# Attention scores on one core: bf16 three-part stacks of 72 rows against two-part fp32r stacks of 26 rows per head, placed in 32-row groups of the array

## The chip, the cores and the metric

The kernel runs on one core of a Trainium2 chip. The metric is the device time of one execution in microseconds (us); lower is better.

## The reference

One layer: attention, layer norm, a mixture of experts (8 routed, 2 chosen, 1 shared), layer norm. Input `x` is (8, 512, 128) in float32.

```python
qkv = (x @ w_qkv + b_qkv).reshape(B, 16, S, 24)          # 16 heads of 8, B=8, S=512
q, k, v = jnp.split(qkv, 3, axis=-1)
attn = softmax(einsum('bhqd,bhkd->bhqk', q, k) / sqrt(8))
vals = einsum('bhqk,bhkd->bhqd', attn, v).transpose(0, 2, 1, 3).reshape(B, S, 128)
x = layernorm(x + vals @ w_out + b_out)
# then the mixture of experts on x, and a second layernorm
```

The reshape makes a "head" out of 32 neighbouring tokens of 128 values, so a tile of 128 tokens holds the whole of 4 heads with 512 queries and 512 keys each.

## The kernel before

The work is cut into 32 tiles of 128 tokens (four heads each, `QUADS`), and the engines' programs are written out by hand as a pipeline of stages. The first part of the kernel (attention) ends at about 508 us; the experts and the last norm follow and are not touched.

A stage `(b, i)` works on several tiles at once, each at another step. With q = 4b + i:

- Tile q + 4: its x is transposed (`xT`, slot 4) and multiplied to Q and K (`qkv`, slot 6). ScalarE copies the product to `qk32`, GpSimd splits it into parts of lower precision (`parts`, L814 to L820).
- Tile q + 3: SyncE (SP) stores `parts` to DRAM (L745), waits for that store, and loads it back as two operand stacks `qs` and `ks` (L756, L760). TensorE waits for all of these loads (`stack_loaded`) at the start of the next stage.
- Tile q + 2: scores A. TensorE multiplies (L980) into `scoreA`, and VectorE takes the maximum over the keys (L923, 1024 values per partition and instruction). The negated maxima become two further rows of `qs` (`m2`, L596 and L598, sent by ScalarE's DMA queue, L898).
- Tile q: scores B with the maxima subtracted (L994), with keys on the partitions, into `scoreB`; ScalarE takes the exponential (L889).
- Tile q - 1: probabilities times V (L1014, float32, four heads in four 32-column groups of the array), "PV" below.

A stage has 8 slots (`at`). In each slot TensorE issues two matmuls A and two matmuls B; after that come the jobs of the slot through one shared bank (`pe_job`: xT, qkv, mT, valsT, proj, oT, x1T, gate, counts), and in odd slots PV. `scoreA` has two halves, so the A of a slot waits for the maximum of two slots before (`max_done`); B waits for the exponential of the matmul two before (`exp_done`). VectorE also does the norm statistics and, from stage 8 on, the routing (`choose`, `place`). Each engine executes its own program strictly in order.

A score product in float32 quality is made in bf16 of three parts of q and k: six products of parts, stacked along the contraction dimension, 3 x 24 = 72 rows (B: 74, with the maxima). One SP load makes one band of rows for all four heads, 8 loads per tile.

## Time and profile before

| what | value |
|---|---|
| median of 3 runs | 753.06 us (752.21 to 755.68) |
| span of the profiled execution | 752.8 us |
| TensorE (PE) busy in the span | 671.8 us, 89% |
| VectorE (DVE) busy | 542.0 us, 72% |
| ScalarE (ACT) busy | 433.5 us, 58% |
| GpSimd (POOL) busy | 286.4 us, 38% |
| mean share of the DMA engines in the stretch 126 to 473 us | 37% |

Busy times of an engine are sums of its instructions without overlap. A matmul's row gives its latency, which overlaps with the next matmul: what it occupies is the distance between two starts. The shares are means over stages with different limits, so the stretches have to be read one by one.

### The profile page before, as it was taken

The numbers are of one execution on the slowest core, as the hardware profiler recorded it, in microseconds if no ns is written. First come the engines' busy times: TensorE is split into PE (matmuls) and PEld (weight loads), VectorE is DVE, ScalarE is ACT, GpSimd is POOL, SyncE is SP. The second block draws the span as 40 slices with busy tenths as digits, with TensorE's granted clock in tenths as the row PEclk, the third lists the DMA queues.
The fourth block names the chain that finished last, engine by engine and source line by source line (L and its number), as shares of the span: only waits on it lengthen the run. The fifth ranks groups of instructions, "written<-read, shape, count | busy, mean of one in ns | idle before, by whom it ended". The sixth has DMA issues, their size and how long they took to land. (4 is left out here: it accounts for less than half of the span.)

```text
span 752.8 us, 17081 instructions
## 1 busy us (share of the span) xinstructions
PE 671.8 (89%) x4621; PEld 322.5 (43%) x4622; DVE 542.0 (72%) x1201; ACT 433.5 (58%) x973; POOL 286.4 (38%) x491
## 2 busy tenths in 40 slices
PE   2899999999999999999999999889989888888334
PEld 1232334334343333333333332328877666666211
DVE  4967777889979979979979989756856444545125
ACT  1066677676767667767667776744325444544106
POOL 2133132223434333343352352242435555555506
PEclk9999999999999999999999999999999999999758
DMA  4357776543342342343243241050122222222044
GB/s 79 78 131 153 151 146 114 107 96 68 74 106 53 66 112 60 55 113 70 48 102 90 46 88 55 3 152 22 40 58 66 63 62 62 63 63 58 13 168 168
DMA packets 161848, 62.57 MB, mean 83 GB/s; under 512 B 110586, under 2 KB 155516, under 8 KB 161808
## 3 DMA queue, kind: packets, MB, share of 16 engines
q1 hardware_dynamic: 154112, 48.55, 29.2%
q0 software_dynamic: 5648, 13.26, 6.0%
q10 hardware_dynamic: 2048, 0.27, 0.3%
q8 instruction: 20, 0.33, 0.2%
q14 instruction: 20, 0.16, 0.1%
HBM read 38.04 MB, written 24.26 MB: 83 GB/s over the span
## 5 line engine op out<-in xcount | busy, mean ns | idle before, releaser
L923 DVE TENSOR_REDUCE mx<-scoreA 128x2 f32<-128x1024 f32 x256 | 305.7, 1220 | 66.7 <-PE scoreA L980 64.2
L889 ACT ACTIVATE prob<-scoreB 128x512 f32<-128x512 f32 x512 | 279.3, 600 | 115.9 <-PE scoreB L994 111.4
L980 PE MATMUL scoreA<-ks,qs 72*128 72x512 bf16 x512 | 205.2, 408 | 12.2 <-DMA ks<-parts_dram 9.6
L994 PE MATMUL scoreB<-qs,ks 74*128 74x512 bf16 x512 | 200.3, 394 | 6.3 <-ACT prob L889 3.0
L1014 PE MATMUL pvp<-prob,v 128*32 128x512 f32 x1024 | 138.1, 612 | 0.8 <-ACT pv_sb L881 0.8
L980 PEld LDWEIGHTS scoreA<-ks,qs 72*128 72x128 bf16 x512 | 50.9, 102 | 152.8 <-DVE mx L923 73.6
L1136 POOL DMA_INDIRECT y_dram<-prob x72 | 70.2, 975 | 72.8 <-ACT prob L1290 58.2
L814 POOL CAST parts<-qk 128x256 bf16<-128x256 f32 x32 | 12.6, 395 | 214.0 <-ACT v_raw L563 195.2
L994 PEld LDWEIGHTS scoreB<-qs,ks 74*128 74x128 bf16 x512 | 49.7, 98 | 101.9 <-ACT prob L889 79.7
L488 POOL DMA_INDIRECT slots_dram<-rows,slot_i x64 | 63.3, 989 | 27.2 <-issue 17.7
L1245 DVE TENSOR_TENSOR prob<-scoreA,prob 128x256 f32<-128x256 f32 x72 | 30.6, 425 | 46.3 <-ACT prob L1284 46.3
L1284 ACT ACTIVATE prob<-scoreA 128x256 f32<-128x256 f32 x72 | 27.6, 383 | 39.4 <-PE scoreA L1386 37.7
L1407 PE MATMUL scoreB<-w,prob 128*128 x288 | 44.1, 276 | 0.1
L1290 ACT ACTIVATE prob<-scoreB,prob 128x128 f32<-128x128 f32 x72 | 26.4, 367 | 23.1 <-PE scoreB L1407 23.1
L1407 PEld LDWEIGHTS scoreB<-w,prob 128*128 128x128 f32 x288 | 37.8, 192 | 0.3 <-issue 0.3
L1384 PE MATMUL scoreA<-w_high,ebT_high 128*128 x72 | 35.2, 489 | 2.7 <-issue 1.7
L1232 DVE TENSOR_TENSOR ebT_low<-scoreA,ebT_high 128x128 fp32r<-128x128 f32 x72 | 20.8, 291 | 22.8 <-ACT ebT_high L1274 21.7
L1501 PE MATMUL scoreA<-prob,ident 128*128 128x512 f32 x28 | 15.1, 708 | 23.1 <-DMA prob<-y_dram 23.1
L1366 PE MATMUL scoreA<-ident,prob 128*128 128x128 f32 x72 | 22.6, 316 | 14.5 <-DMA prob<-slots_dram 14.1
L1014 PEld LDWEIGHTS pvp<-prob,v 128*32 128x32 f32 x1024 | 20.5, 109 | 29.3 <-issue 27.7
L1512 ACT ACTIVATE prob<-prob 128x128 f32<-128x128 f32 x32 | 13.2, 482 | 32.9 <-POOL prob L1491 32.9
L1250 DVE COPY prob<-pvp 128x256 f32<-128x256 f32 x72 | 29.9, 415 | 0.6 <-PE pvp L1394 0.6
(177 smaller groups left out, 911.4 us busy)
## 6 DMA issues: line engine op xcount, KB each, us to landing
qs<-parts_dram SPq DMA_DIRECT2D x96, 96.0 KB
parts_dram<-parts SPq DMA_DIRECT2D x32, 192.0 KB, 3.7
slots_dram<-blank POOLq DMA_DIRECT2D x9, 520.0 KB
prob<-slots_dram SPq DMA_DIRECT2D x72, 65.0 KB, 1.8
ks<-parts_dram SPq DMA_DIRECT2D x64, 64.0 KB
prob<-y_dram SPq DMA_DIRECT2D x8, 512.0 KB, 4.4
ks<-parts_dram SPq DMA_DIRECT2D x32, 96.0 KB
xin<-in_L_attn_x SPq DMA_DIRECT2D x32, 64.0 KB, 2.1
```

What stands on the lines that cost most here:

```text
L488: pool.indirect_dma_start(slots_dram, bass.IndirectOffsetOnAxis(ap=slot_i[:, j, t:t + 1], axis=0), rows[:, t, j, :], None).then_inc(scatte ...
L889: act.activation(prob[:, i % 2, j, 2 * u + c, :], scoreB[:, c], ACT.Exp, scale=SCALE).then_inc(exp_done, 1)
L923: dve.tensor_reduce(mx[:, i % 2, at // 2, at % 2 * 2:at % 2 * 2 + 2], scoreA[:, at % 2], AX.X, ALU.max).then_inc(max_done, 1)
L980: ins = pe.matmul(scoreA[:, at % 2, c], qs[0:KR, st, j, qc * P:(qc + 1) * P], ks[0:KR, st, j, :], start=True, stop=True)
L994: pe.matmul(scoreB[:, c], ks[0:KM, i, j, kc * P:(kc + 1) * P], qs[0:KM, i, j, :], start=True, stop=True).then_inc(b_ready, 1)
L1014: ins = pe.matmul(pvp[32 * h:32 * h + 32, :], v[:, (i - 1) % 2, h, j, :], prob[:, (i - 1) % 2, h, j, :], start=(j == 0), stop=(j == 3))
L1136: pool.indirect_dma_start(y2_dram, bass.IndirectOffsetOnAxis(ap=yrow_i[:, r:r + 1], axis=0), yo[:, r, :], None, bounds_check=TOP_K * TILES ...
L1245: dve.tensor_tensor(gated[:, r % 2, :], scoreA[:, 0, r % 2, F:2 * F], silu[:, r % 2, :], ALU.mult) \
L1250: dve.tensor_copy(gatedT[:, (r - 1) % 2, :], pvp[:, 0:F]).then_inc(gT_copied, 1)
L1284: act.activation(silu[:, r % 2, :], scoreA[:, 0, r % 2, 0:F], ACT.Silu).then_inc(silu_done, 1)
L1384: pe.matmul(h, ebT_high[:, r % 2, 0:P], high, start=True, stop=False)
L1407: ins = pe.matmul(y, gatedT[:, r % 2, c * P:(c + 1) * P], w2_flat[:, bass.ds(e * NFC * D + c * D, D)], start=(c == 0), stop=(c == NFC - 1))
```

## The change

q and k are split into two fp32r parts instead of three bf16 parts. Three products of parts are stacked: 24 rows per head (B: 26 with the maxima) instead of 72. Each head's stack lies in its own 32 partitions (`GROUP`), so that the four heads lie beside each other in `qs` and `ks`, and a score matmul uses 32 rows of the array's 128. The two A matmuls of a slot are now those of two heads (2 and 3 in slots 0 to 3, then 0 and 1), each in its own row group, and are issued one behind the other; the two B matmuls (of one head) follow. GpSimd's split has two instructions instead of four. SP makes the stacks with 16 loads of 8 or 16 rows per tile instead of 8 of 8 to 24 rows. Not shown: the maxima's two rows are written as fp32r, and the four memsets that put ones into `ks` cover 128 partitions of 512 float32 values instead of 32 partitions of 2048 bf16 values.

```diff
@@ -110,12 +110,9 @@
-    KR = 9 * HD
-    PR = 3 * HD
-
-    K_ROWS = [(0, 0, 3), (PR, 1, 3), (PR + 2 * HD, 0, 1), (2 * PR, 2, 3), (2 * PR + HD, 0, 2)]
-    STACK_DMAS = 3 + len(K_ROWS)
+    KR = 3 * HD
     KM = KR + 2
+    GROUP = 32
     NE = E + 1
...
@@ -139,7 +136,7 @@
-        parts_dram = nc.dram_tensor("parts_dram", (2, 2, 4, 3, P, 32), BF16).ap()
+        parts_dram = nc.dram_tensor("parts_dram", (2, 2, 4, 2, P, 32), F32).ap()
...
@@ -169,12 +166,14 @@
         qk32 = sb("qk32", [P, 2, 4, 32])
-        qkr = sb("qkr", [P, 2, 4, 32])
-        parts = sb("parts", [P, 2, 4, 3, 32], BF16)
-        qs = sb("qs", [P, 4, 4, 512], BF16)
-        ks = sb("ks", [P, 4, 4, 512], BF16)
+        parts = sb("parts", [P, 2, 4, 2, 32], F32R)
+        qs = sb("qs", [P, 4, 512], F32R)
+        ks = sb("ks", [P, 4, 512], F32R)
+
+        STACK = ((0, qs, 0, 0, 1), (0, qs, HD, 0, 2), (1, ks, 0, 0, 2), (1, ks, 2 * HD, 0, 1))
+        STACK_DMAS = 4 * len(STACK)
         mx = sb("mx", [P, 2, 4, NCH])
-        m2 = sb("m2", [16, 2, P], BF16)
+        m2 = sb("m2", [16, 2, P], F32R)
...
@@ -743,7 +743,7 @@
                     need(sp, stack_loaded[par], 16 * STACK_DMAS * (2 * b + (i + 3) // 2))
                     sp.dma_start(parts_dram[par].rearrange("k h i p t -> p (k h i) t"),
-                                 parts[:].rearrange("p k h i t -> p (k h i) t")).then_inc(parts_stored, 16)
+                                 parts[:].rearrange("p k h i t -> p (k h i) t").bitcast(F32)).then_inc(parts_stored, 16)
                     need(sp, parts_stored, 16 * (n + 1))
                     if has(b, i, -1):
...
@@ -752,14 +752,11 @@
                     if isinstance(b, int) and n < 4:
                         sp.wait_ge(ones_set, n + 1)
-                    for r in range(3):
-                        sp.dma_start(qs[PR * r:PR * (r + 1), st],
-                                     parts_dram[par, 0].rearrange("h i (d c) t -> (i d) h (c t)", d=HD)) \
-                          .then_inc(stack_loaded[par], 16)
-                    for row, i0, i1 in K_ROWS:
-                        sp.dma_start(ks[row:row + HD * (i1 - i0), st],
-                                     parts_dram[par, 1, :, i0:i1].rearrange("h i (d c) t -> (i d) h (c t)", d=HD)) \
-                          .then_inc(stack_loaded[par], 16)
+                    for k, to, row, i0, i1 in STACK:
+                        for h in range(4):
+                            sp.dma_start(to[GROUP * h + row:GROUP * h + row + HD * (i1 - i0), st].bitcast(F32),
+                                         parts_dram[par, k, h, i0:i1].rearrange("i (d c) t -> (i d) (c t)", d=HD)) \
+                              .then_inc(stack_loaded[par], 16)
...
@@ -812,12 +809,8 @@
                     need(pool, parts_stored, 16 * n)
                     need(pool, split_done, n)
                     pool.tensor_copy(parts[:, :, :, 0, :], qk32[:]).then_inc(split_step, 1)
-                    need(pool, split_step, 3 * n + 1)
-                    pool.tensor_tensor(qkr[:], qk32[:], parts[:, :, :, 0, :], ALU.subtract).then_inc(split_step, 1)
-                    need(pool, split_step, 3 * n + 2)
-                    pool.tensor_copy(parts[:, :, :, 1, :], qkr[:]).then_inc(split_step, 1)
-                    need(pool, split_step, 3 * n + 3)
-                    pool.tensor_tensor(parts[:, :, :, 2, :], qkr[:], parts[:, :, :, 1, :], ALU.subtract) \
+                    need(pool, split_step, n + 1)
+                    pool.tensor_tensor(parts[:, :, :, 1, :], qk32[:], parts[:, :, :, 0, :].bitcast(F32), ALU.subtract) \
                         .then_inc(split_done, 1)
                 if isinstance(b, int) and q == -4:
                     columns_of_blanks()
...
@@ -920,8 +913,9 @@
                 for at in range(8):
                     if has(b, i, 2):
                         dve.wait_ge(a_ready, 8 * (q + 2) + at + 1)
-                        dve.tensor_reduce(mx[:, i % 2, at // 2, at % 2 * 2:at % 2 * 2 + 2], scoreA[:, at % 2], AX.X,
-                                          ALU.max).then_inc(max_done, 1)
+                        h = FIRST_A[at // 4]
+                        dve.tensor_reduce(mx[:, i % 2, h:h + 2, at % 4], scoreA[:, at % 2], AX.X, ALU.max) \
+                           .then_inc(max_done, 1)
                     for kind in jobs.at(b, i, at):
                         if kind in ("valsT", "proj", "mT"):
                             dve_job(dve, kind, b, i)
...
@@ -970,17 +964,17 @@
                 if has(b, i, 2):
                     pe.wait_ge(stack_loaded[i % 2], 16 * STACK_DMAS * (2 * b + i // 2 + 2))
-                def score_a(at, c):
+                def score_a(at):
                     if has(b, i, 2):
-                        st, j, qc = (i + 2) % 4, at // 2, at % 2 * 2 + c
-
-                        if c == 0:
-                            need(pe, max_done, 8 * (q + 2) + at - 1)
-                        ins = pe.matmul(scoreA[:, at % 2, c], qs[0:KR, st, j, qc * P:(qc + 1) * P],
-                                        ks[0:KR, st, j, :], start=True, stop=True)
-                        if c == 1:
-                            ins.then_inc(a_ready, 1)
+                        st, qc = (i + 2) % 4, at % 4
+
+                        need(pe, max_done, 8 * (q + 2) + at - 1)
+                        for c in range(2):
+                            g = GROUP * (FIRST_A[at // 4] + c)
+                            ins = pe.matmul(scoreA[:, at % 2, c], qs[g:g + KR, st, qc * P:(qc + 1) * P],
+                                            ks[g:g + KR, st, :], start=True, stop=True)
+                        ins.then_inc(a_ready, 1)
                 def score_b(at, c):
...
@@ -991,14 +985,14 @@
                             pe.wait_ge(m_loaded, 32 * (q + 1))
                         need(pe, exp_done, 16 * q + 2 * at + c - 1)
-                        pe.matmul(scoreB[:, c], ks[0:KM, i, j, kc * P:(kc + 1) * P], qs[0:KM, i, j, :],
+                        g = GROUP * j
+                        pe.matmul(scoreB[:, c], ks[g:g + KM, i, kc * P:(kc + 1) * P], qs[g:g + KM, i, :],
                                   start=True, stop=True).then_inc(b_ready, 1)
                 for at in range(8):
                     j, u = at // 2, at % 2
-                    score_a(at, 0)
+                    score_a(at)
                     score_b(at, 0)
-                    score_a(at, 1)
                     score_b(at, 1)
                     for kind in jobs.at(b, i, at):
                         pe_job(pe, kind, b, i)
```

TensorE's program, the first two slots of a stage, before (L980 is scores A, L994 scores B, L521 the transposed maxima, L1014 PV; in brackets the semaphores it waits for):

```order
L980 MATMUL scoreA<-ks,qs 128x512 [waits max_done,stack_loaded1]
L994 MATMUL scoreB<-qs,ks 128x512 [waits exp_done,m_loaded]
L980 MATMUL scoreA<-ks,qs 128x512
L994 MATMUL scoreB<-qs,ks 128x512 [waits exp_done]
L980 MATMUL scoreA<-ks,qs 128x512 [waits max_done]
L994 MATMUL scoreB<-qs,ks 128x512 [waits exp_done]
L980 MATMUL scoreA<-ks,qs 128x512
L994 MATMUL scoreB<-qs,ks 128x512 [waits exp_done]
L521 MATMUL shared<-ident,mx 16x128 [waits max_done,job_read]
L1014 MATMUL pvp<-prob,v 32x512 [waits v_ready,exp_done]
L1014 MATMUL pvp<-prob,v 32x512 x3
```

and the same place of the changed kernel (L975 is scores A, L989 scores B, L1008 PV):

```order
L975 MATMUL scoreA<-ks,qs 128x512 [waits max_done,stack_loaded1]
L975 MATMUL scoreA<-ks,qs 128x512
L989 MATMUL scoreB<-qs,ks 128x512 [waits exp_done,m_loaded]
L989 MATMUL scoreB<-qs,ks 128x512 [waits exp_done]
L975 MATMUL scoreA<-ks,qs 128x512 [waits max_done]
L975 MATMUL scoreA<-ks,qs 128x512
L989 MATMUL scoreB<-qs,ks 128x512 [waits exp_done] x2
L521 MATMUL shared<-ident,mx 16x128 [waits max_done,job_read]
L1008 MATMUL pvp<-prob,v 32x512 [waits v_ready,exp_done]
L1008 MATMUL pvp<-prob,v 32x512 x3
```

The number of matmuls is the same; the second A of a slot stands ahead of the first B, and no longer behind its wait. SP's program for one tile, before:

```order
L745 DMA parts_dram<-parts 128x24x32
L756 DMA qs<-parts_dram 24x4x512 x3
L760 DMA ks<-parts_dram 24x4x512
L760 DMA ks<-parts_dram 16x4x512
L760 DMA ks<-parts_dram 8x4x512 x2
L760 DMA ks<-parts_dram 16x4x512
```

and in the changed kernel (L757 is the one line of all loads):

```order
L745 DMA parts_dram<-parts 128x16x32
L757 DMA qs<-parts_dram 8x512 x4
L757 DMA qs<-parts_dram 16x512 x4
L757 DMA ks<-parts_dram 16x512 x4
L757 DMA ks<-parts_dram 8x512 x4
```

One load per head and band takes the place of one load per band: 16 issues instead of 8, with 3072 pieces of 128 bytes instead of 9216 of 64.

## Rows read from the trace of the kernel before

**Rows 1.** Busy us (and instructions) by stretch; PEclk, DMA share, GB/s at the end.

```profile
0.00:56.00 56.00, 39.08 (x159) 14.75 (x161) 37.93 (x40) 16.38 (x36) 13.31 (x32) 1.00 0.44 94
56.00:126.00 70.00, 69.69 (x531) 23.88 (x530) 51.77 (x58) 49.90 (x107) 19.77 (x44) 1.00 0.72 144
126.00:473.00 347.00, 343.59 (x2696) 131.35 (x2698) 306.84 (x620) 242.56 (x515) 123.30 (x198) 1.00 0.37 79
```

**Rows 2.** Groups by line, 241 to 299 us: busy us, mean ns, idle before.

```profile
L923 DVE TENSOR_REDUCE mx<-scoreA 128x2 f32<-128x1024 f32 x33 | 39.4, 1220 | 6.0 <-PE scoreA L980 5.5
...
L994 PE MATMUL scoreB<-qs,ks 74*128 74x512 bf16 x64 | 24.6, 384 | 0.4
...
L1014 PE MATMUL pvp<-prob,v 128*32 128x512 f32 x128 | 17.0, 605 | 0.0
```

**Rows 3.** TensorE in order of time, from 306.58 us: start, duration, x instructions.

```profile
306.58 1.07 PE L1014 MATMUL pvp<-prob,v 128*32 128x512 f32 x8
307.58 0.39 PE L980 MATMUL scoreA<-ks,qs 72*128 72x512 bf16 x1
307.80 0.38 PE L994 MATMUL scoreB<-qs,ks 74*128 74x512 bf16 x1
```

**Rows 4.** Groups by line and shape of TensorE, 42 to 57 us.

```profile
L994 PE MATMUL scoreB<-qs,ks 74*128 74x512 bf16 x16 | 10.1, 634 | 0.0
```

**Rows 5.** TensorE in order of time, 57 to 61 us.

```profile
56.98 0.63 PE L980 MATMUL scoreA<-ks,qs 72*128 72x512 bf16 x1
57.41 0.63 PE L994 MATMUL scoreB<-qs,ks 74*128 74x512 bf16 x1
...
58.19 1.94 PE L1014 MATMUL pvp<-prob,v 128*32 128x512 f32 x8
60.05 0.47 PE L980 MATMUL scoreA<-ks,qs 72*128 72x512 bf16 x1
```

**Rows 6.** Busy time and granted clock (PEclk) of two short stretches.

```profile
508.00:510.70 2.70, 1.76 (x12) 1.50 (x12) 0.38 (x2) 2.37 (x3) 0.48 (x4) 1.00 0.03 6
511.00:514.00 3.00, 3.00 (x12) 2.54 (x11) 1.45 (x6) 0.11 (x1) 0.00 (x0) 0.50 0.00 0
```

**Rows 7.** All engines in order of time, 516 us: matmuls of fp32r operands.

```profile
516.23 0.40 PE L1354 MATMUL scoreA<-ebT_high,w_high 128*128 128x512 f32 x1
516.23 0.19 PEld L1355 LDWEIGHTS scoreA<-ebT_high,w_low 128*128 128x128 f32 x1
516.46 0.39 PE L1355 MATMUL scoreA<-ebT_high,w_low 128*128 128x512 f32 x1
```

**Rows 8.** All engines in order of time, 300 to 317 us.

```profile
300.09 0.39 PE L980 MATMUL scoreA<-ks,qs 72*128 72x512 bf16 x1
...
301.72 0.38 SPq L745 DMA_DIRECT2D parts_dram<-parts  x1
...
305.71 1.14 SPq L756 DMA_DIRECT2D qs<-parts_dram  x3
...
306.89 1.94 SPq L760 DMA_DIRECT2D ks<-parts_dram  x5
...
311.56 0.38 PE L509 MATMUL shared<-xT,wq 128*128 128x128 f32 x2
...
313.23 0.28 ACT L563 ACTIVATE v_raw<-shared 128x128 f32<-128x128 f32 x1
...
313.93 0.40 POOL L814 CAST parts<-qk 128x256 bf16<-128x256 f32 x1 [1.21 <-ACT v_raw L563]
...
316.85 0.38 SPq L745 DMA_DIRECT2D parts_dram<-parts  x1
```

**Rows 9.** All engines in order of time, 12 to 18 us.

```profile
13.66 1.83 SPq L760 DMA_DIRECT2D ks<-parts_dram  x5
...
17.72 0.61 PE L980 MATMUL scoreA<-ks,qs 72*128 72x512 bf16 x1 [9.35 <-DMA ks<-parts_dram]
```

**Rows 10.** ScalarE's copy of PV, once a stage; duration min/median/max, first and last start.

```profile
L881 ACT ACTIVATE pv_sb<-pvp x31: 597/597/598, 70.3 to 500.0; 128x512 f32<-128x512 f32 x31
```

More of the change, by code:

```diff
@@ L284, in layer @@
         CHOSEN = 14
+        FIRST_A = (2, 0)
         PLACED = 38
@@ L597, in dve_job @@
                 need(dve, msplit_step, q + 2)
-                dve.scalar_tensor_tensor(m2[:, 1, :], shared[0:16, 0:P], -1.0, m2[:, 0, :], ALU.mult,
+                dve.scalar_tensor_tensor(m2[:, 1, :], shared[0:16, 0:P], -1.0, m2[:, 0, :].bitcast(F32), ALU.mult,
                                          ALU.subtract).then_inc(job_read, 1)
@@ L897, in stage @@
                             for m in range(2):
-                                act.dma_start(qs[KR + m:KR + m + 1, (i + 1) % 4].rearrange("p h x -> p (h x)"),
-                                              m2[:, m, :]).then_inc(m_loaded, 16)
+                                act.dma_start(qs[KR + m::GROUP, (i + 1) % 4].bitcast(F32),
+                                              m2[:, m, :].bitcast(F32)).then_inc(m_loaded, 16)
             run_stages(act, stage)
@@ L951, in _ @@
             dve.memset(v[:], 0.0).then_inc(cleared, 1)
-            dve.memset(ks[64:96, 0], 1.0).then_inc(ones_set, 1)
-            dve.memset(ks[64:96, 1], 1.0).then_inc(ones_set, 1)
+            dve.memset(ks[:, 0].bitcast(F32), 1.0).then_inc(ones_set, 1)
+            dve.memset(ks[:, 1].bitcast(F32), 1.0).then_inc(ones_set, 1)
             dve.memset(half[:], -0.5).then_inc(cleared, 1)
@@ L957, in _ @@
             dve.memset(blank[:], 0.0).then_inc(cleared, 1)
-            dve.memset(ks[64:96, 2], 1.0).then_inc(ones_set, 1)
-            dve.memset(ks[64:96, 3], 1.0).then_inc(ones_set, 1)
+            dve.memset(ks[:, 2].bitcast(F32), 1.0).then_inc(ones_set, 1)
+            dve.memset(ks[:, 3].bitcast(F32), 1.0).then_inc(ones_set, 1)
             dve.wait_ge(cleared, CLEARS)
```

## The prediction

> **What bounds the kernel now.** I read the busy times by stretch first. Between 56 and 126 us TensorE (PE) is busy 69.7 of 70.0 us and VectorE (DVE) 51.8 (74%); between 126 and 473 us, where norms and routing are added, PE is busy 343.6 of 347.0 us and DVE 306.8 (88%) [rows 1]. So PE looks like the only limit, but DVE stands close behind it. ScalarE copies PV once a stage, 31 times from 70.3 to 500.0 us: 14.3 us a stage [rows 10]. The view by lines of four of these stages says who waits: in 58 us the maxima are 39.4 us of DVE's work, and in front of them DVE stands idle 6.0 us, 5.5 of them for scores A [rows 2]. These 6.0 us per four stages are all that a faster PE can give where routing runs; then DVE is the limit.
>
> What PE's time consists of is read from the distances between starts. A score matmul occupies 0.22 us (307.58 to 307.80) and a PV group of eight instructions 1.00 us (306.58 to 307.58) [rows 3]. Per stage: 32 scores are 7.0 us, 4 PV groups 4.0 us, and in the plain stretch (five stages in 70 us, 14.0 each) 3.0 us remain for the jobs.
>
> TensorE's clock decides as much. The page's clock column shows nothing low before 470 us, but the durations do: from 42 to 57 us the scores B take 634 ns [rows 4] against 384 ns later [rows 2], and their starts lie 0.43 us apart [rows 5], twice the 0.22. That is the 1.2 GHz level. PE streamed scores there without a gap and the clock did not rise; it rose behind the first PV group: 58.19 us at the low level, and the next matmul A at 60.05 us is already of the short kind [rows 5]. Near the end it is seen the other way round: from 508 to 510.7 us PE is busy only 1.76 us of 2.70, and in the next row the granted clock is 0.50 [rows 6].
>
> **The change, part by part.**
>
> Rate of fp32r. Matmuls of 512 columns with fp32r operands start 0.23 us apart, their weight loads take 0.19 us and lie under the matmul before them, on the same rows (516.23 and 516.23) [rows 7]. Against 0.22 that is nothing: 32 x 0.01 = 0.3 us a stage, on PE alone.
>
> Two heads at once. The two A of a slot lie in different row groups and write different banks. The trace shows no row groups, but it shows column groups: the eight PV instructions, each over 512 columns, take 1.00 us together [rows 3], where one after another at 0.22 they would take at least 1.76. I take the same for rows. The third group, of the first B, can run beside them or not: a slot then costs between 2 x 0.23 = 0.45 us and 3 x 0.22 = 0.66 us, where it was 0.88; a stage 3.6 to 5.3 us where it was 7.0. If nothing overlaps it stays at 7.4 us (a rival below).
>
> Switching. PV takes 1.00 us at the high clock and 1.86 at the low [rows 3, 5]; with a part that doubles and a part that doesn't, 0.86 doubles and 0.14 is fixed. That fixed part I charge for each change between row groups, column groups and the whole array. Jobs in even slots, and behind the scores in odd ones, now bring about six more: 0.8 us a stage. Net on PE: 7.0 - (3.6 to 5.3) - 0.8 - 0.3 = 0.6 to 2.3 us less a stage. In the plain stretch a stage of PE's own work is then 11.7 to 13.4 us.
>
> The Trainium skill (page "TensorE: Matmul & The Clock Gate", Part 3 on packing) says that a weight load overlaps running matmuls only where the row group differs. The two B of a slot share one; by that rule 8 x 0.19 = 1.5 us a stage would come back and eat most of the gain. The trace disagrees: the load at 516.23 runs under a matmul on the same 128 rows [rows 7], and the measurement decides.
>
> DVE. Number and length of the maxima stay (33 x 1220 ns) [rows 2]. The floor of four stages is 58 - 6 = 52 us. PE will not hide everything: behind slot 6 it has the qkv job and then a PV group before the next A, over 2 us against the 1.22 of a maximum. I take 60% of the 6.0 us: 3.6 us per four stages, and with 347 / 58 = 6 groups **-22 us** (bounds: 0 and -36).
>
> The way of the stacks. From the start of the qkv job in one stage to the matmul two stages later that needs it: 311.56 to 313.93 is 2.4 us to GpSimd's cast; 2.9 to SP's store (316.85); store to first load 4.0 (301.72 to 305.71); eight loads 3.1 (1.14 and 1.94) [rows 8]; last issue to TensorE 2.2 (15.49 to 17.72) [rows 9]. Sum 14.6; qkv stands 11.5 us into its stage (300.09 to 311.56) [rows 8], and 2 x 14.3 - 11.5 = 17.1 are there: 2.5 us to spare. Afterwards: two of four split instructions, -1.4; eight more issues at 0.39, +3.1: 16.3. With qkv about 9 us into a shorter stage (six maxima of 1.22 us and the small jobs between them), a stage can't be shorter than (9 + 16.3) / 2 = 12.7 us. That is under DVE's floor with routing (13.0 and up), so it costs nothing there, but it limits the plain stretch: five stages from 14.0 to 12.7, **-6 us** (0 to -9).
>
> The start. The first A waits for the first stack (17.72) [rows 9]: +3.1 - 1.4 = +1.7 us. The stage of 42 to 57 us, 32 x 0.43 = 13.8 us of scores, falls to 8 slots x 3 x 0.43 = 10.3: -3.4. With the later stacks of the stages between I set the sum to 0 (-2 to +2). The larger memsets, the maxima's two rows and the stored bytes lie off the path; fewer and longer DMA pieces only help (DMA share 0.72 and 0.37) [rows 1]. The last stages have no A: 0.
>
> The clock. With 26 of 128 rows at work and PE waiting for DVE, the array does much less than before, and rows 5 and 6 say that this is what the clock follows. I expect it to fall now and then. Price: at the low level a stage of PE is 8 x (0.86 to 1.29) + 4 x 1.86 + 2 x 3.0 = 20 to 24 us against 13.6, so 7 to 10 us for each stage's worth spent low. I take a stage and a quarter of some 29, in short pieces: **+10 us** (bounds 0 and, all of them low, +200 to +290).
>
> The skill's same page (Part 1, the clock gate) says the grant follows how busy TensorE has been; by it alone a PE above 90% busy would keep its clock, and the sum would be 10 us lower. The row of 42 to 57 us, without a gap at 634 ns, says that busy time alone isn't it [rows 4].
>
> Sum: 752.8 (span; 0.3 us from the median of the runs) - 22 - 6 + 0 + 10 = **735 us**. With the bounds of the first terms and a clock that hardly falls: 708 to 748.
>
> **The rivals.**
>
> Slower, by the clock (0.19). For: the scores were 57% of the array's rows and become 20%, PE gets gaps, and low it stayed through 15 us of dense scores [rows 4]. Against: PV, behind which it rose, stays as it is, and when PE gets slower it has fewer gaps again. It decides from 28 / (7 to 10) = 3 to 4 stages' worth low. Seven stages low give 725 + 50 to 70 = 775 to 795; half of them 830 and more.
>
> Row groups don't run at once (0.08). Then PE keeps its 32 x 0.23 and pays the switches, 0.3 + 0.8 = 1.1 us a stage, in 29 stages +32: 785 us.
>
> The stacks come late (0.07). If a load costs 0.5 us of SP or lands later, the way is 18 us and more, a stage 13.6 to 14.2: 742 to 750 us.
>
> PE's gain is real, but DVE's waits only move to other places (0.06): 749 to 756, no change.
>
> **How the numbers follow.** The forecast holds 0.60. Differences under 0.5% (3.8 us, 749.3 to 756.8) can't be told from none. Faster: 0.60 and 0.04 of the late stacks = 0.64. No change: 0.03 + 0.06 = 0.09. Slower: 0.19 + 0.08 = 0.27. The range runs from 706 (two more than the best forecast) to 800, which leaves out the longer half of the clock's rival and little else.
>
> **What would show it.** Right: both A of a slot starting within 0.2 us of each other, with the next matmul of the whole array at 0.5 to 0.7 us after a slot's start; DVE busy 93% or more between the same stages, its idle time before the maxima near 2.4 us in four stages; plain stages of 12.5 to 13 us; scores of 0.4 us with short stretches of 0.63. Wrong: A starts 0.23 us apart (no overlap); scores and PV at 0.63 and over 1 us for long stretches, and granted clock of 0.5 inside the attention (clock); TensorE waiting for `ks` or `qs` loads at a stage's start (stacks).

## The result

The changed kernel takes 840.94 us (831.8 to 867.63, 4 runs) against 753.02 us before. The ratio is 1.105 [1.0982, 1.1118]: slower; it is taken over fast runs alone, those within 1.5% of the kernel's fastest (here 831.8 and 836.67 us). The forecast was 735 us, range 706 to 800; the time lies outside the range, on the side of the rival "slower, by the clock". The profiled execution is the 831.8 us run, span 830.0 us, beside the span of 752.8 us before.

The page after: engine totals, the slices with TensorE's granted clock, and the groups that answer to [rows 2].

```profile
PE 727.4 (88%) x4621; PEld 360.1 (43%) x4622; DVE 541.9 (65%) x1201; ACT 435.0 (52%) x973; POOL 255.7 (31%) x427
...
PEclk9999999976975998988988965556999999999958
...
L917 DVE TENSOR_REDUCE mx<-scoreA 128x2 f32<-128x1024 f32 x256 | 305.4, 1221 | 122.6 <-PE scoreA L975 120.6
...
L989 PE MATMUL scoreB<-qs,ks 26*128 26x512 f32 x512 | 248.4, 555 | 21.3 <-ACT prob L882 20.7
L1008 PE MATMUL pvp<-prob,v 128*32 128x512 f32 x1024 | 177.7, 775 | 0.8 <-ACT pv_sb L874 0.8
L975 PE MATMUL scoreA<-ks,qs 24*128 24x512 f32 x512 | 142.6, 582 | 15.7 <-DMA ks<-parts_dram 11.9
```

The clock row, in which the page of before has no digit under 9 ahead of its 38th slice (696 us), is now broken from its 9th slice on (166 us). A mean hides this at first sight: PV is 775 ns over the whole span here, where it was 605 in [rows 2]. It is a mixture of about 605 and 1062. By stretches it comes apart:

```profile
56.00:106.00 50.00, 48.52 (x242) 17.00 (x241) 24.72 (x29) 23.63 (x48) 6.32 (x17) 1.00 0.49 108
318.00:369.00 51.00, 48.64 (x421) 21.07 (x417) 44.81 (x91) 36.38 (x79) 14.15 (x23) 1.00 0.27 59
369.00:379.00 10.00, 9.19 (x37) 3.00 (x34) 7.35 (x16) 4.51 (x9) 4.08 (x5) 0.50 0.45 97
495.00:570.00 75.00, 72.48 (x342) 26.06 (x341) 37.98 (x100) 34.37 (x66) 17.59 (x24) 0.50 0.10 23
```

The first of these rows prints 1.00, but that stands there only because the trace has no record of the clock before 106 us; the durations say that it was low (the same trap as in [rows 4] against [rows 1]). TensorE by line and shape, 60 to 100 us of the changed kernel:

```profile
L989 PE MATMUL scoreB<-qs,ks 26*128 26x512 f32 x31 | 19.3, 719 | 1.2 <-ACT prob L882 1.2
L1008 PE MATMUL pvp<-prob,v 128*32 128x512 f32 x64 | 15.5, 1062 | 0.0
L975 PE MATMUL scoreA<-ks,qs 24*128 24x512 f32 x30 | 10.8, 756 | 0.0
```

PV takes 1062 ns and B 719: the 1.2 GHz level until 106 us, where before it ended at 60 us [rows 5]. By the records of the clock it then falls every 20 to 70 us, for 10 to 31 us, and from 495 to 570 us it is low throughout. Of the 513 us from the first to the last of the matmuls below it is low for 226.

Stage lengths are the distances between the starts of the matmul that transposes the maxima (L521), one a stage:

| | before | after |
|---|---|---|
| stages 1 to 6, us | 12.5 15.6 14.3 13.6 13.6 13.6 | 12.9 13.7 20.0 21.1 16.8 13.6 |
| four stages from 326.3 (after) and 287.3 us (before) | 15.5 13.7 15.2 13.7 | 15.0 13.7 16.0 16.7 |
| last three | 15.2 13.2 14.9 | 21.9 19.9 23.1 |
| start of the 7th / 29th / 32nd of these matmuls | 113.1 / 432.9 / 476.2 | 127.9 / 477.9 / 542.8 |
| first matmul of the experts' loop (L1366, now L1360) | 557.3 | 635.4 |

So the 78 us are lost in four places: 14.8 in the first stages, 30.2 over the 22 stages of the middle, 21.6 in the last three, 11.5 behind them, where norms and the last PV still run low. From there to the end both take 195 us. Every stage that is more than 0.3 us longer has a low clock in it. The stages wholly at the high clock take what they took before: 13.6 or 13.7, and at best 0.5 less (15.0 for 15.5).

### The profile page after: what moved, and what is told of

It is laid out like the page before. It is cut to its first block and busy times, and to the rows that moved or that the text cites. A ratio compares the mean times of both kernels' runs of the same rounds, so it can differ in the third digit from the quotient of the medians.

```text
span 830.0 us, 17193 instructions
## 1 busy us (share of the span) xinstructions
PE 727.4 (88%) x4621; PEld 360.1 (43%) x4622; DVE 541.9 (65%) x1201; ACT 435.0 (52%) x973; POOL 255.7 (31%) x427
## 2 busy tenths in 40 slices
DMA packets 119096, 58.65 MB, mean 71 GB/s; under 512 B 79098, under 2 KB 106620, under 8 KB 119056
## 5 line engine op out<-in xcount | busy, mean ns | idle before, releaser
L989 PE MATMUL scoreB<-qs,ks 26*128 26x512 f32 x512 | 248.4, 555 | 21.3 <-ACT prob L882 20.7
L1008 PE MATMUL pvp<-prob,v 128*32 128x512 f32 x1024 | 177.7, 775 | 0.8 <-ACT pv_sb L874 0.8
L975 PE MATMUL scoreA<-ks,qs 24*128 24x512 f32 x512 | 142.6, 582 | 15.7 <-DMA ks<-parts_dram 11.9
L989 PEld LDWEIGHTS scoreB<-qs,ks 26*128 26x128 f32 x512 | 101.5, 225 | 93.1 <-ACT prob L882 77.5
L975 PEld LDWEIGHTS scoreA<-ks,qs 24*128 24x128 f32 x512 | 54.7, 222 | 158.2 <-issue 74.1
L811 POOL CAST parts<-qk 128x256 fp32r<-128x256 f32 x32 | 12.6, 395 | 287.8 <-ACT v_raw L563 266.3
L1284 ACT ACTIVATE prob<-scoreB,prob 128x128 f32<-128x128 f32 x72 | 26.5, 368 | 23.1 <-PE scoreB L1401 22.8
L1008 PEld LDWEIGHTS pvp<-prob,v 128*32 128x32 f32 x1024 | 22.4, 120 | 34.4 <-issue 30.5
L1226 DVE TENSOR_TENSOR ebT_low<-scoreA,ebT_high 128x128 fp32r<-128x128 f32 x72 | 20.9, 291 | 22.9 <-ACT ebT_high L1268 21.6
L1360 PE MATMUL scoreA<-ident,prob 128*128 128x128 f32 x72 | 22.5, 314 | 14.6 <-DMA prob<-slots_dram 14.0
L559 ACT ACTIVATE qk<-shared,bq 128x128 f32<-128x128 f32 x64 | 20.1, 364 | 19.9 <-PE shared L514 14.5
```

Of the source, the lines that this page charges most:

```text
L975: ins = pe.matmul(scoreA[:, at % 2, c], qs[g:g + KR, st, qc * P:(qc + 1) * P], ks[g:g + KR, st, :], start=True, stop=True)
L989: pe.matmul(scoreB[:, c], ks[g:g + KM, i, kc * P:(kc + 1) * P], qs[g:g + KM, i, :], start=True, stop=True).then_inc(b_ready, 1)
L1008: ins = pe.matmul(pvp[32 * h:32 * h + 32, :], v[:, (i - 1) % 2, h, j, :], prob[:, (i - 1) % 2, h, j, :], start=(j == 0), stop=(j == 3))
```

## The experiments

A job's own runs of the kernel before were 756, 776, 775 or 775 us, so only ratios are compared over jobs; stage lengths come from the profiles. Of the runs taken once, stage lengths alone are used. Every stage length is that of one profiled execution.

**e1: rows alone.** The kernel before with its scores over 24 of the 72 rows; nothing else is changed. Two thirds of the products and the maxima's rows are left out.

```diff
-                        ins = pe.matmul(scoreA[:, at % 2, c], qs[0:KR, st, j, qc * P:(qc + 1) * P],
-                                        ks[0:KR, st, j, :], start=True, stop=True)
+                        ins = pe.matmul(scoreA[:, at % 2, c], qs[0:PR, st, j, qc * P:(qc + 1) * P],
+                                        ks[0:PR, st, j, :], start=True, stop=True)
...
-                        pe.matmul(scoreB[:, c], ks[0:KM, i, j, kc * P:(kc + 1) * P], qs[0:KM, i, j, :],
+                        pe.matmul(scoreB[:, c], ks[0:PR, i, j, kc * P:(kc + 1) * P], qs[0:PR, i, j, :],
```

> The kernel before with one thing changed: the score matmuls A and B use rows 0 to 23 of their stacks instead of 72 and 74 (it leaves out two thirds of the products and the maxima); still bf16, still no row groups, the same number of matmuls, columns and loads. Theory (the clock follows how much of the array works, and the changed kernel lost it by its 24 to 26 rows): the clock falls here too, scores of 0.63 us appear in long stretches; as nothing overlaps, a low stage is about 23 us against 14.3, and the time is 830 us or more. Rival (fp32r operands, or the row groups, bring the clock down, not the number of rows): no fall, 750 to 756 us.

Measured: 930.74 us, ratio 1.2093 [1.1991, 1.2195]. TensorE's totals in its windows, and its lines in the same stretch:

```profile
56.00:168.00 112.00, 112.00 (x458) 29.44 (x457) 49.36 (x55) 49.77 (x93) 19.26 (x42) 1.00 0.47 91
L994 PE MATMUL scoreB<-qs,ks 24*128 24x512 bf16 x72 | 45.3, 629 | 0.0
...
L1014 PE MATMUL pvp<-prob,v 128*32 128x512 f32 x144 | 34.8, 1062 | 0.0
```

TensorE has no gap in 112 us, with the instructions of before, and the clock stays low: PV takes 1062 ns, and the 1.00 in the row stands only for want of a record before 168 us. A low stage takes 25.3 us (about 23 forecast). After 168 us the clock alternates, and a plain stage at the high level takes 14.1. bf16, no row groups, no new order: fewer rows are enough to lose the high clock here, and TensorE being busy without a gap did not raise it.

**e14: rows given back.** The changed kernel with scores B over all 128 rows.

```diff
-                        g = GROUP * j
-                        pe.matmul(scoreB[:, c], ks[g:g + KM, i, kc * P:(kc + 1) * P], qs[g:g + KM, i, :],
+                        pe.matmul(scoreB[:, c], ks[:, i, kc * P:(kc + 1) * P], qs[:, i, :],
...
+            dve.memset(qs[:, 0].bitcast(F32), 0.0)
             dve.memset(ks[:, 0].bitcast(F32), 1.0).then_inc(ones_set, 1)
```

(and the same memset for the other three parts of `qs`)

> The changed kernel with scores B over all 128 rows of the stacks instead of the 26 of one head; the sum then holds the scores of the four heads (the probabilities are those of that sum), with the instructions, stacks, loads, maxima and exponentials as in the changed kernel. Theory (the clock follows how many rows are at work, not fp32r, nor the 32-row groups, nor the waits): the clock rises near 60 us as before and stays until the last stages; a stage takes 13.6 to 14.3 us where it is plain; ratio 1.00 to 1.03. It gives no gain over before, since the exponentials hold the scores B back. Rival (fp32r stacks, the paired A or the gaps bring the clock down whatever the rows): above 1.08, with falls as in the changed kernel.

Measured: 808.32 us, ratio 1.0406 [1.0332, 1.048]. The page's clock row and the long stretch of [rows 1]:

```profile
PEclk9999999999999999999999999998999999999858
126.00:473.00 347.00, 345.29 (x2481) 157.56 (x2480) 284.64 (x565) 229.21 (x478) 94.20 (x142) 1.00 0.31 66
```

The clock rises at 63 us (before: 60) and does not fall until 541 us. fp32r, row groups for A, paired A and the loads are those of the changed kernel, so none of them is enough to bring the clock down. The edit does two things, though: it gives rows back, and as B now overlaps with no A, TensorE also has hardly a gap (345.29 of 347 us busy; the changed kernel 48.64 of 51). That it is the closed gaps that hold the clock is not excluded by this run; e1 speaks against it, with no gap in 112 us and the clock low. The forecast of no loss was too good: plain stages take 15.1 us, not 13.6 to 14.3, for B over all rows lies beside no A:

```profile
92.67 0.50 PE L979 MATMUL scoreA<-ks,qs 24*128 24x512 f32 x2
93.10 0.73 PE L992 MATMUL scoreB<-qs,ks 128*128 128x512 f32 x2
93.76 0.50 PE L979 MATMUL scoreA<-ks,qs 24*128 24x512 f32 x2
```

Its B starts 0.43 us behind the A, and the slot takes 1.09 us (92.67 to 93.76), where that of before took 0.88. Its two B over all rows take 0.66 us (93.10 to 93.76), as much as the pair in one row group does (below). This kernel has a high clock and is still slower than before.

**e13: the order alone.** The kernel before with two heads at a time and the order A, A, B, B.

```diff
-                        st, j, qc = (i + 2) % 4, at // 2, at % 2 * 2 + c
+                        st, j, qc = (i + 2) % 4, (2, 0)[at // 4] + c, at % 4
...
                     score_a(at, 0)
-                    score_b(at, 0)
                     score_a(at, 1)
+                    score_b(at, 0)
```

> One part of the change alone: the kernel before (bf16 stacks of 72 rows) with the two A of a slot of two heads and issued one behind the other (A, A, B, B). Theory: every matmul still uses more than half of the array, so the clock stays high from about 60 us on; the order costs or gives nothing that can be told, 748 to 758 us on a chip where before takes 753 (ratio 0.99 to 1.01). Rival (it is the order A, A, B, B with its waits that makes TensorE's clock fall in the changed kernel): falls inside the attention and 5% or more.

Measured: 781.93 us, ratio 1.0087 [1.0055, 1.0119], clock high from 67 us on. With stacks of 72 rows the order has no part in the clock. It costs a little, at the edge of what I expected: plain stages 14.3 instead of 13.6 us.

**e5: the order undone.** The changed kernel, but A, B, A, B.

```diff
-                    score_a(at)
+                    score_a(at, (0,))
                     score_b(at, 0)
+                    score_a(at, (1,))
                     score_b(at, 1)
```

> The changed kernel with the slot's matmuls in the old order: A of the first head, B, A of the second head, B. Read from its stages at the high clock, since the clock falls here too. Theory (a slot at the high clock is long because the two B lie in one row group, each waiting for its own weight load, 0.33 us apart, and because B waits for the exponentials; the A beside them costs nothing): the stages stay within 0.3 us of the changed kernel's 13.6 to 15.0 us. Rival (the second A in front of the first B delays the exponentials and took the gain): stages shorter by 0.5 us or more.

One run of 854.97 us, clock falling as in the changed kernel. Its plain stages at the high clock are 13.5 us, so in the changed kernel the order is not what holds them at 13.6.

**e10, e11, e12: who holds the stage at the high clock.** Shorter exponentials in the changed kernel (e10) and before (e11), shorter maxima in the changed kernel (e12).

```diff
+                                W = 512 if isinstance(b, int) and q < 2 else 256
-                                act.activation(prob[:, i % 2, j, 2 * u + c, :], scoreB[:, c], ACT.Exp,
+                                act.activation(prob[:, i % 2, j, 2 * u + c, 0:W], scoreB[:, c, 0:W], ACT.Exp,
```

```diff
-                        dve.tensor_reduce(mx[:, i % 2, h:h + 2, at % 4], scoreA[:, at % 2], AX.X, ALU.max) \
+                        dve.tensor_reduce(mx[:, i % 2, h:h + 2, at % 4], scoreA[:, at % 2, :, 0:256], AX.X, ALU.max) \
```

> The changed kernel with exponentials of 256 instead of 512 columns from the third tile on (half of the probabilities are left out). Theory: at the high clock TensorE's scores B wait for the exponentials through the two banks of scoreB, and this has taken the place of TensorE's own work as the limit; four exponentials of 0.6 us stand against two slots of 0.66 us. Halved, they are some 0.33 us, and a plain stage that lies wholly at the high clock falls from 13.6 us by 1.0 us or more. Rival (TensorE's own work and switching fill the stage in the changed kernel too): 13.3 to 13.6 us. Both expect a lower clock for much of the time.

> The kernel before with the same halved exponentials. By both theories TensorE's own work is the limit there, and its plain stages stay at 13.4 to 13.6 us. If they fall by more than 0.5 us, the exponentials were part of the limit before the change too, and TensorE was never alone on the path.

> The changed kernel with maxima over 256 instead of 512 keys per head (half of the keys are left out of the maximum). Theory (exponentials limit): plain stages at the high clock stay at 13.4 to 13.6 us, and only the stages with routing, 15.2 to 16 us, get shorter. Rival (the maxima limit through the two halves of scoreA): plain stages fall by 1 us or more.

A plain stage wholly at the high clock takes 12.3 us in e10, 13.0 in e11, 13.6 in e12. The windows of these stages, e10, e11, e12 (PE, PEld, DVE, ACT, POOL busy, as in [rows 1]):

```profile
93.20:105.50 12.30, 11.70 (x107) 4.86 (x106) 10.43 (x13) 6.60 (x22) 2.32 (x4) 1.00 0.64 139
```

```profile
85.20:98.20 13.00, 13.00 (x108) 4.84 (x106) 10.45 (x13) 7.41 (x22) 3.35 (x8) 1.00 0.68 149
```

```profile
156.40:170.00 13.60, 12.64 (x107) 4.97 (x107) 7.94 (x21) 9.94 (x22) 3.66 (x6) 1.00 0.40 81
```

Halved exponentials (384 for 597 ns) take 1.3 us from the changed kernel's stage. Halved maxima take nothing: VectorE's work is down to 7.94 us, and the stage stays. So the exponentials bound the plain stage. With them halved TensorE is busy 11.70 of 12.30 us and is close behind as the next limit. Before, TensorE looks like the limit, busy 13.53 of 13.60 us; but with halved exponentials (e11) the stage fell there too, by 0.6, below the 13.4 to 13.6 that I had put down. The exponentials held it as well.

The second half of what I expected of e12 missed, and it teaches more. A stage with routing should have got shorter with shorter maxima. The same kind of stage, wholly at the high clock, in the changed kernel and in e12:

```profile
326.30:341.30 15.00, 14.57 (x123) 6.76 (x122) 13.70 (x32) 10.31 (x23) 3.67 (x7) 1.00 0.31 62
```

```profile
268.10:283.10 15.00, 14.56 (x123) 6.76 (x122) 8.99 (x30) 10.32 (x23) 3.71 (x7) 1.00 0.33 62
```

VectorE has 4.7 us less to do, and the stage stays at 15.0 us. Of the four kinds of stage that alternate behind 126 us this is the one with the most work for VectorE. VectorE does not bound it. Nor does VectorE bound the shortest kind: it takes 13.7 us in the changed kernel and in e12, and 12.4 in e10.

**e2 and e9: rows without use.** Two extra matmuls of 128 rows ahead of the A of each odd slot (e2); in e9 also three in every slot of the first stages.

```diff
+                        for _ in range(FILLERS[at % 2]):
+                            pe.matmul(scoreA[:, at % 2, 0], ks[:, st, 0:P], ks[:, st, :], start=True, stop=True)
                         for c in range(2):
```

(`FILLERS` is (0, 2); e9 has `range(3 if isinstance(b, int) and b < 1 else FILLERS[at % 2])`)

> The changed kernel with two further matmuls over all 128 rows and columns (fp32r, 512 columns, result overwritten) ahead of the two A of each odd slot, where TensorE otherwise waits about 0.5 us for the exponentials: 8 a stage, 0.22 us each. Theory: the array works more, the clock stays high, and since at the high clock the stages are as long as before (13.6 to 15 us), the time falls from 832 to 752 to 765 us. Rival (the stages are long for another reason, the low clock is only a sign of waiting): 830 us or more, since the work only grows.

> The run with two extra matmuls before the scores A of each odd slot held its high clock from 172 us on, but its stages up to there took 23.5 to 24.5 us. Here the first stages (up to the A of stage (0, 3)) get three extra matmuls of 128 rows in every slot, the rest as in that run. Theory (the clock follows the work of the array's rows): the clock rises in the first stages, before 100 us, and stays; stages as in that run at the high clock, 14.3, 15.9, 14.3 and 16.6; time 770 to 795. It is then still above before, though the clock is high, since the change gives no time back at the high clock and the extra matmuls cost 0.7 us a stage. Rival (the late rise is random, not a matter of the work in the first stages): low until 150 us or later, 825 and more.

e2: 828.83 to 894.45 us, median 861.66 (before 756.13). Expected 752 to 765, missed. Two lines from 60 to 160 us, and the stretch behind the rise:

```profile
L992 PE MATMUL scoreB<-qs,ks 26*128 26x512 f32 x68 | 41.4, 707 | 0.0
L1011 PE MATMUL pvp<-prob,v 128*32 128x512 f32 x128 | 31.0, 1062 | 0.0
172.00:476.00 304.00, 300.45 (x2408) 131.82 (x2404) 256.56 (x501) 207.56 (x433) 85.75 (x130) 1.00 0.32 69
```

Low until 172 us, at 23.5 to 24.5 us a stage, then high for 304 us. e4 below, with the same extra matmuls and a copy on ScalarE, rose at 99 us, and fell again for 120 us at 331: the extra matmuls do not hold the clock reliably. e10, whose first stages are those of the changed kernel, rose at 86 us where that rose at 106. With one profile of each, such moments can't be compared closely. e9: 849.3 us, ratio 1.0989 [1.0904, 1.1075]; the clock rose at 81 us, as expected (beside e4's 99 and e10's 86 that is weak evidence), and fell for 20 us at 217. The time is 54 us above my range: the three extra matmuls made the first stages 17.4 to 21.1 us, so that the sixth of the L521 matmuls starts at 137.9 us (the changed kernel: 114.2). The later ones cost 0.7 us a plain stage (14.3) and more where routing runs, up to 15.1 for 13.7. The last stages were at the high clock, but behind them, between 559 and 589 us, it was low for 27 us. Work added to hold the clock cost what it gave.

**e3: the overlap taken away.** e2 with both A of a slot in the row group of the same head as B.

```diff
-                            g = GROUP * (FIRST_A[at // 4] + c)
+                            g, qc = GROUP * j, at % 2 * 2 + c
```

> As the run with the fillers, but the two A of a slot are again of one head, the same as that of the B of the slot, so that all four lie in one row group and none can overlap. Theory (at the high clock the overlap gives almost nothing, because TensorE waits for the exponentials anyway): within 15 us of the run with the fillers. Rival (the overlap is worth its 0.2 us and more a slot on the path, 1.7 us a stage, and something else took the gain): 50 us or more above it.

1111.11 to 1189.66 us, median 1177.83: my theory, which gave the overlap no worth, missed. Stages at the high clock are 17.5 us and more (e2: 14.3), low ones 31.3 (24.5). The row groups do run at once, and it is worth some 3 us a stage against the same stacks without it. TensorE's four score matmuls of a slot in one row group, with the weight loads (PEld) of the last two:

```profile
331.53 0.73 PE L977 MATMUL scoreA<-ks,qs 24*128 24x512 f32 x2
331.87 0.42 PEld L991 LDWEIGHTS scoreB<-qs,ks 26*128 26x128 f32 x2
332.10 0.63 PE L991 MATMUL scoreB<-qs,ks 26*128 26x512 f32 x2
332.66 0.33 PE L504 MATMUL shared<-ident,xin 128*128 128x128 f32 x1
```

They take 1.13 us, where those of bf16 take 0.88. So of what the overlap gives, a part only makes up for that.

**e4: the exponentials' turn.** e2 with a copy on ScalarE, 0.2 to 0.25 us, between the two exponentials of even slots.

```diff
+                                if u == 0 and c == 1:
+                                    act.activation(extra[:], ident[:, 0:64], ACT.Copy)
```

> As the run with the fillers, with one short ScalarE copy (128x64, some 0.2 us) between the two exponentials of each even slot: 4 a stage, 128 in all. Theory (ScalarE's exponentials, two banks of scores B, are the path through a pair of slots): the whole of it shows, 4 x 0.2 x 29 = 20 to 25 us more than the run with the fillers. Rival (VectorE or TensorE's own work sets the stage): 0 to 5 us more.

824.24 to 873.7 us, median 858.06, which says nothing beside e2's spread. Stages at the high clock 14.8, 16.4, 14.8, 16.6 against e2's 14.3, 15.9, 14.3, 16.6: half of the added 0.8 to 1.0 us in three of four stages, nothing in the fourth, where I had expected the whole. ScalarE is on the path there, but with slack left in places.

**e6, e8: PV between the two B of odd slots,** in the changed kernel (e6) and on e7's kernel (e8), so that ScalarE has work during PV. **e7:** the kernel before with B over 128 rows, the added ones zero.

```diff
+                    if u == 1:
+                        pv(j)
                     score_b(at, 1)
```

```diff
-                        pe.matmul(scoreB[:, c], ks[0:KM, i, j, kc * P:(kc + 1) * P], qs[0:KM, i, j, :],
+                        pe.matmul(scoreB[:, c], ks[:, i, j, kc * P:(kc + 1) * P], qs[:, i, j, :],
...
+            dve.memset(qs[64:128, 0], 0.0)
```

> The changed kernel with PV of an odd slot between the slot's two B instead of behind them and the jobs, so that the exponential of the first B runs under PV. Read from its stages at the high clock. Theory (TensorE and ScalarE wait for each other in a pair of slots: TensorE about 0.5 us for the exponentials in front of B, ScalarE about 1 us during PV): the plain stage falls from 13.6 to 12.4 to 13.0 us. Rival (TensorE's own work or VectorE sets the stage): 13.4 us or more. The clock falls as in the changed kernel or a little less; no time is forecast from it.

> The kernel before with scores B over all 128 rows of the stacks instead of 74; rows 74 to 127 of qs are zeros, so the result is the same, and a matmul takes as long. Theory (the clock follows how much of the array works): it rises soon after the first B, some 42 to 50 us instead of 60, and as TensorE is the limit there, the kernel gains a half of that: 744 to 750 us. Rival (zero rows don't count, or it is PV as such, a float32 matmul, that raises the clock): it rises at 60 us as before, 751 to 754 us.

> As the run with B over 128 rows on the kernel before, with PV of an odd slot between the slot's last A and last B. Theory (in front of B TensorE waits for the exponentials, some 0.2 us twice in an odd slot, and ScalarE stands idle under PV): 0.3 to 0.6 us a stage less, 10 to 20 us below the run without the move. Rival (at the high clock TensorE's own work sets the stage, or VectorE with routing): within 4 us of it.

e6, one run: 1022.12 us, a mean clock of 0.691. Its one stage wholly at the high clock (168.6 to 183.3 us) takes 14.7 us, where the changed kernel's takes 13.6 and I had expected 12.4 to 13.0: a miss. e8: 794.7 us, 1.0207 [1.0135, 1.0279], a miss; plain stages 14.7 instead of 13.6 or 13.7. The place of PV is worse in both by some 1 us, and I did not find out by which wait. e7: 772.19 us, 0.9941 [0.9894, 0.9987]. Its clock was high from 44 to 54 us already, and then from 61 as before; e8, with the same B, shows the same. It is the only version that came out ahead of before, by about half a per cent. That B over 128 rows brings the clock up earlier is suggested by these two, not shown; and the half per cent does not come from there in the profile, where the seventh of the L521 matmuls starts at 113.1 us, as before.

## Why the prediction was wrong

**The clock term (+10) was mis-sized, and that decides.** The price of a low stage was right: 20 to 24 us forecast, 19.9 to 23.1 measured, against 13.6 to 14.9. The extent was not. I took "a stage and a quarter of some 29"; lost are 78 us, 66.6 of them in the stages, at 6.4 to 8.2 us a stage some eight to ten stages' worth, and 11.5 behind the last scores. I had read the right rows ([rows 4] and [rows 5]: 15 us of dense scores without a rise) and said that the array would do much less. Then the sum let it fall "now and then". The step that was missing is a comparison: in the row of 42 to 57 us 72 rows at work and no gap did not raise the clock, and the changed kernel's scores use 24 or 26. PV as such does not hold it up either: e1 has the same PV and 24 rows, and stays low for 112 us. With two thirds of the scores' rows gone a low clock had to be expected for much of the attention (it was 226 of 513 us), not now and then. That fewer rows bring the clock down is shown by e1; e14 brings it back by more rows, with the gaps closed at the same time. The start shows it most plainly. I credited the stage of 42 to 57 us with 3.4 us for shorter scores. It did get 1.9 shorter (15.6 to 13.7), but the rise came 46 us later, and the first six stages together lost 14.8.

The Trainium skill (page "TensorE: Matmul & The Clock Gate", Part 1) ties the grant to how busy TensorE is. Here 112 us with TensorE busy 112.00 of them stayed at 1.2 GHz in e1; setting the rule aside was right, and the consequence was drawn too small. The rival "slower, by the clock" (0.19) is what happened; that the other terms gave nothing back brought the time to its longer half. The bounds 708 to 748 do not come out of the terms, which give 705.8 to 754.8 with a clock that hardly falls. The miss does not hang on that.

**The gain of -22 us (and -6 in plain stages) did not come.** The step that failed is "60% of the 6.0 us", and with it "then DVE is the limit": it assumed that TensorE's shorter slots reach VectorE and that VectorE sets the stage. In e12 the stage with routing kept its 15.0 us with VectorE's work cut from 13.70 to 8.99, and the plain one its 13.6. Two slots of the changed kernel at the high clock, without PV between them, and ScalarE in the same stretch:

```profile
342.54 0.50 PE L975 MATMUL scoreA<-ks,qs 24*128 24x512 f32 x2
342.55 0.49 PE L989 MATMUL scoreB<-qs,ks 26*128 26x512 f32 x1
342.88 0.39 PE L975 MATMUL scoreA<-ks,qs 24*128 24x512 f32 x1
342.88 0.39 PE L989 MATMUL scoreB<-qs,ks 26*128 26x512 f32 x1
342.88 0.39 PE L975 MATMUL scoreA<-ks,qs 24*128 24x512 f32 x1
343.77 0.99 PE L989 MATMUL scoreB<-qs,ks 26*128 26x512 f32 x2 [0.49 <-ACT prob L882]
344.69 0.66 PE L525 MATMUL shared<-ident,pv_sb 128*128 128x128 f32 x4
345.27 1.06 PE L1008 MATMUL pvp<-prob,v 128*32 128x512 f32 x8
346.27 0.50 PE L975 MATMUL scoreA<-ks,qs 24*128 24x512 f32 x2
```

```profile
343.12 2.27 ACT L882 ACTIVATE prob<-scoreB 128x512 f32<-128x512 f32 x4 [0.97 <-PE scoreB L989]
...
346.84 1.09 ACT L882 ACTIVATE prob<-scoreB 128x512 f32<-128x512 f32 x2 [1.45 <-PE scoreB L989]
```

The first slot lasts 342.54 to 342.88, its A and the first B starting within 0.01 us. The second issues its A at 342.88, and then B stands 0.49 us for `prob`: both banks of `scoreB` are full. The two slots end at 344.69, after 2.15 us. The same two slots in the kernel before:

```profile
86.98 0.39 PE L980 MATMUL scoreA<-ks,qs 72*128 72x512 bf16 x1
...
87.86 0.38 PE L980 MATMUL scoreA<-ks,qs 72*128 72x512 bf16 x1
88.28 0.39 PE L994 MATMUL scoreB<-qs,ks 74*128 74x512 bf16 x1
88.50 0.38 PE L980 MATMUL scoreA<-ks,qs 72*128 72x512 bf16 x1
88.77 0.39 PE L994 MATMUL scoreB<-qs,ks 74*128 74x512 bf16 x1
89.00 0.38 PE L525 MATMUL shared<-ident,pv_sb 128*128 128x128 f32 x2
```

2.02 us, 86.98 to 89.00, of which 8 x 0.22 = 1.76 are needed: the B at 88.28 stands 0.42 us behind the A before it, and the one at 88.77 0.27. Such waits are shorter than a matmul's latency, so they hide in TensorE's busy time. Four exponentials take 2.27 us without a gap (343.12), more than the scores of two slots need in either kernel. Behind them ScalarE stands idle 1.45 us, until PV (345.27 to 346.27) and the next slot's first matmuls are through. A plain stage of the changed kernel in its windows, and one of before:

```profile
114.20:127.90 13.70, 12.73 (x108) 5.03 (x107) 10.55 (x13) 9.93 (x22) 2.11 (x4) 1.00 0.51 120
```

```profile
85.80:99.40 13.60, 13.53 (x107) 4.74 (x106) 10.40 (x13) 9.88 (x22) 3.30 (x7) 1.00 0.75 142
```

ScalarE is busy 9.93 us and waits 3.8, nearly all of it for `scoreB`, as before (9.88 of 13.60). TensorE's own work did shrink, from 13.53 to 12.73 us, within my 11.7 to 13.4; the 0.8 us became waiting for `prob` (1.0 us ahead of B in this stage). Idle time of VectorE ahead of the maxima is the sign that I had named: 5.8 us in 51 us,

```profile
L917 DVE TENSOR_REDUCE mx<-scoreA 128x2 f32<-128x1024 f32 x29 | 34.7, 1219 | 6.2 <-PE scoreA L975 5.8
L882 ACT ACTIVATE prob<-scoreB 128x512 f32<-128x512 f32 x56 | 30.5, 598 | 14.9 <-PE scoreB L989 14.3
L989 PE MATMUL scoreB<-qs,ks 26*128 26x512 f32 x58 | 24.0, 468 | 1.6 <-ACT prob L882 1.4
```

where I expected 2.4 in four stages; [rows 2] had 6.0 in 58. In its outcome this is what the smallest rival (0.06) described, at the high clock; but it named VectorE's waits, not the exponentials. The evidence was in the trace of before, in the view of waits of 241 to 299 us:

```profile
ACT prob L889 <- PE scoreB L994: 12.9, 13, 1.4
PEld scoreB L994 <- ACT prob L889: 8.3, 20, 0.6
```

ScalarE waits 12.9 us for `scoreB` and TensorE's weight loads wait 8.3 us for `prob`, each for the other. The prediction asked only who waits for TensorE. e10 and e12 show the limit of the plain stage by moving it, and e11 that the exponentials held it before too.

**Row groups run at once: right.** Both A and the first B start together (above), a slot with room costs 0.66 us (122.31 to 122.97) where it cost 0.88, the upper end of my 0.45 to 0.66. **The weight load within one row group: right, with a price overlooked.** I set the rule of the Trainium skill (page "TensorE: Matmul & The Clock Gate", Part 3) aside by [rows 7]. By that rule matmuls of one row group would start some 0.23 + 0.18 = 0.41 us apart (an estimate). In e3, with four in one row group, the first B starts 0.23 us behind the second A (331.87 and 332.10), its load under the A; the trace does not bear the rule out there either. Only the second matmul behind a wait or a change starts later, 0.34 us after the first (331.53 and 331.87). That has nothing to do with the row group: the two B of a slot start 0.33 us apart in the changed kernel (342.55 and 342.88), and as far apart in e14 over the whole array. I had read 0.23 from the middle of a run ([rows 7]), but here a slot's two B are a run of two, and the second pays 0.1 us more: 0.8 us a stage.

**The stacks: right in that they cost nothing.** The first A starts at 18.40 us, 0.7 later than in [rows 9] (forecast +1.7), and in the 51 us from 318 TensorE waits for no load. DMA packets fall from 161848 to 119096, which gave nothing that these runs show.

**What remains open.** Why the falls come just when they do: those at 307.5, 368.9 and 430.3 us are 61.4 us apart, the length of the four stages between them, so it is a matter of the place in the program; ahead of the fall at 368.9 TensorE is busy 13.5 of 13.9 us. Why PV between the two B costs a microsecond (e6, e8); and why the kernel before took 20 us more in some jobs. The exponentials' bound was shown at plain stages and at the shortest of the four kinds behind 126 us. What bounds the kind of 15.0 us is open: not VectorE (e12), and before not the exponentials either, for with them halved (e11) it takes 15.4 to 15.7 us, as before.

## What to carry to other kernels

Before cutting the rows of a matmul look for a stretch of the trace in which TensorE streams without a gap and the clock is low all the same. Where there is one, put a low clock for much of the kernel into the sum, and try the cut of rows alone first, as e1 does: here it cost 21% by itself. Where two engines pass two banks between them, read both directions of the waits, and remember that a wait shorter than a matmul's latency shows only in the distances between starts; a faster producer gives nothing while the consumer's turn plus the break is as long. And a clock that is shown as 1.00 ahead of the first record is no reading: take a duration that you know at both levels.

## What the runs showed of the hardware that was not expected

- TensorE stayed at 1.2 GHz through 112 us of gapless matmuls of 24 rows (e1), and rose at 63 us, to stay high until 541, when one half of the score matmuls used 128 rows (e14).
- Matmuls of fp32r in three row groups start within 0.01 us of each other. The second of a run in one row group starts 0.33 to 0.34 us behind the first, later ones 0.23 (e3); over the whole array it is the same (e14, [rows 7]).
- The clock's state at the end of the attention went on into the norms behind it: 11.5 us lost there.
